# Edge scores of a graph attention layer: heads summed on TensorE by one-column products in place of ScalarE's summing passes

## What is computed

```python
out = (x @ Wv + bv)                        # V, 8 heads of 64
e = concat([x[src], x[dst]], axis=1) @ Ww + bw   # 6144 x 1024: 8 heads of 128
e = leaky_relu(e, 0.01)
w = (e @ Wa + ba)                          # Wa: 128 x 1, one score for each edge and head
mat = full((H, n, n), -inf).at[:, src, dst].set(w)
y = softmax(mat) @ out                     # then elu, residual, layernorm
```

## Time and profile before

| what | value |
|---|---|
| runs, median (lowest to highest) | 927.63 us (926.61 to 930.39) |
| the profiled execution, its own time | 931.85 us |
| its span, first to last instruction | 929.8 us |
| PE, busy share of the span | 72% |
| DVE | 59% |
| ACT | 29% |
| POOL | 25% |
| granted TensorE clock, mean | 0.825 |

### The profile page before, as it was taken

How to read it: one execution, slowest core, us unless ns; L and a number is a source line. 1 busy time by engine, 2 the same in 40 slices (tenths; PEclk the granted TensorE clock), 3 DMA queues, 4 the chain that set the end, 5 groups by cost and what they waited for, 6 DMA issues and landing times.

```text
span 929.8 us, 9900 instructions
## 1 busy us (share of the span) xinstructions
PE 664.9 (72%) x3019; PEld 336.2 (36%) x3053; DVE 544.3 (59%) x1452; ACT 273.2 (29%) x1097; POOL 231.4 (25%) x230
## 2 busy tenths in 40 slices
PE   5942443522317808972779989379999999999997
PEld 2421121201106704441355544234444444444442
DVE  2448986887978995448463242644458544444433
ACT  2105764645651312431131010202222222222222
POOL 4154776776852610000000000011110111111000
PEclk9985555755556958995879999769999999999999
DMA  8597576877749149003000000618999999999970
GB/s 336 206 389 271 161 250 210 248 222 238 231 158 336 57 170 406 35 0 136 1 0 1 0 1 0 233 39 331 399 401 398 392 395 401 396 388 400 387 292 36
DMA packets 46215, 208.04 MB, mean 224 GB/s; under 512 B 8128, under 2 KB 12224, under 8 KB 36560
## 3 DMA queue, kind: packets, MB, share of 16 engines
q1 hardware_dynamic: 26624, 145.43, 40.0%
q0 software_dynamic: 19536, 61.95, 20.3%
HBM read 200.45 MB, written 10.05 MB: 226 GB/s over the span
## 4 chain that ended last, share of the span: by engine, by line
PE 51%; DVE 8%; issue 1%; DMA 1%; ACT 1%; DVEq 0%; POOLq 0%
PE bank L781 13%; PE bank L809 7%; PE bank L801 6%; PE bank L693 4%; PE bank L708 3%; PE bank L514 2%; PE bank L615 2%; PE bank L621 2%; PE bank L770 2%; PE bank L509 2%; PE bank L762 1%; DMA R<-tok_tab,slot_tok 1%; PE bank L726 1%; PE bank L723 1%; DVE sm L1074 1%
## 5 line engine op out<-in xcount | busy, mean ns | idle before, releaser
L558 PE MATMUL bank<-R 128*128 128x384 bf16 x144 | 51.0, 490 | 140.5 <-DVE R L1156 110.7
L892 ACT ACTIVATE R<-R 128x128 f32<-128x128 f32 x384 | 113.3, 296 | 104.0 <-DVE R L1195 85.8
L781 PE MATMUL bank<-R 128*64 128x512 f32 x576 | 133.8, 607 | 0.0
L467 POOL DMA_INDIRECT R<-tok_tab,slot_tok x36 | 36.1, 1002 | 301.9 <-DVE slot_f L1546 301.2
L514 PE MATMUL bank<-R,xT_s 128*128 128x512 f32 x168 | 80.5, 640 | 1.9 <-DMA R<-L_Ww 1.9
L892 ACT ACTIVATION_READ_ACCUMULATOR R<-R 128x1 f32 x384 | 72.1, 188 | 13.7 <-issue 13.5
L558 PEld LDWEIGHTS bank<-R 128*128 128x128 bf16 x144 | 13.5, 120 | 173.2 <-DVE R L1156 129.1
L1558 DVE TENSOR_TENSOR R<-R,bank 128x256 f32<-128x256 f32 x36 | 15.1, 421 | 103.0 <-ACT R L972 103.0
L801 PE MATMUL bank<-R 128*64 128x512 f32 x288 | 73.3, 599 | 0.5 <-ACT R L966 0.5
L809 PE MATMUL bank<-R 128*128 128x512 bf16 x291 | 68.7, 379 | 6.3 <-issue 5.1
L427 POOL DMA_INDIRECT score<-w_e,e_i x48 | 59.4, 1238 | 41.7 <-DVE w_e L1150 29.6
(11 more groups left out here) (327 smaller groups left out, 1132.1 us busy)
## 6 DMA issues: line engine op xcount, KB each, us to landing
R<-L_w SPq DMA_DIRECT2D x72, 1536.0 KB, 10.1
R<-L_w SPq DMA_DIRECT2D x2, 3072.0 KB, 15.0
score<-R POOLq DMA_DIRECT2D x9, 512.0 KB, 14.7
R<-score SPq DMA_DIRECT2D x3, 1536.0 KB, 10.3
R<-L_Ww SPq DMA_DIRECT2D x2, 2048.0 KB, 14.6
R<-L_W SPq DMA_DIRECT2D x4, 1024.0 KB, 9.4
tab_src<-R SPq DMA_DIRECT2D x3, 516.0 KB, 2.7
tab_dst<-R SPq DMA_DIRECT2D x3, 516.0 KB
```

The source lines that it names most:

```text
L558: last = pe.matmul(pb[s][:, 0:N], oh[:, e % 2, 0, P * s:P * s + P], oh[:, e % 2, 1, :], start=(e == 0), stop=(e == ET - 1))
L781: last = pe.matmul(pb[4 + i % 2][halves[h], :], xeT[i % 2][:, k, halves[h]], w13[(2 * i + h) % NWB][:, k, :], start=(k == 0), stop=(k == K ...
L892: act_.activation(own, own, ACT.Copy, accum_out=w_e3[:, t, h:h + 1]).then_inc(S("heads_summed"), 1)
```

## The change

- **Tables** are plain: rows of 1024 numbers, `linear_part` and `add_linear` are gone. Target rows are built in three of the gather buffers (`ab_dst`), no longer in the buffers of the source rows.
- **DVE** rectifies in place, max(0.01 z, z) over 1024 columns, and later stores the sums of tile t-2 plus the bias from PSUM (`store_sums`).
- **PE** transposes the 8 heads of each tile (two banks of four), and sums a head by a product of the transposed head as weights with Wa, one column wide (`sum_heads`), one tile behind.
- **ACT** copies the two banks of transposes of each tile to SBUF (`leakyT`), 128x512 each, in place of its 8 passes.
- **V** is projected and gets its bias ahead of the loop. Wv and bv are loaded ahead of the table stores; gamma, beta and the two weights of the later layer after tile 10's scores.
- **Duplicates** are searched in groups of three tiles, each over its own and the previous tile (256 columns), in one bank; no search against the group before is needed.
- **POOL** gathers 10 tiles of source rows at once and four more in the first four tiles, into a ring of 14; a source buffer is free when its transposes are done. The scatter is of tile t-2.

```diff
-ROW = 2 * D + H
-NGF = 13
+ROW = 2 * D
+NGS = 14
+NGA = 10
 NGD = 6
-V_FROM = 4
+KEYS = 3
+Z_BANK = (3, 4, 5, 7)
...
+            sp.dma_start(Wv, a["L0_Wv"].rearrange(chunks, p=P)).then_inc(S("Wv_loaded"), 16)
+            sp.dma_start(bvr, a["L0_bv"].partition_broadcast(P)).then_inc(S("Wv_loaded"), 16)
...
+            sp.wait_ge(S("w_ready"), 10)
+            for row, name in ((g0r, "L0_gamma"), (b0r, "L0_beta")):
+                sp.dma_start(row, a[name].partition_broadcast(P)).then_inc(S("bit_w_loaded"), 16)
...
-                if t >= NGF:
-                    pool.wait_ge(S("rows_added"), t - NGD + 1)
+                if t >= NGS:
+                    pool.wait_ge(S("zT_psum"), 2 * (t - NGS) + 2)
...
             for t in range(ET):
-                if t >= 1:
-                    scatter_score(t - 1)
+                if t >= 2:
+                    scatter_score(t - 2)
                 if t + 4 < ET:
                     gather_dst(t + 4)
-                if NGF <= t + 4 < ET:
+                if t < NGS - NGA:
+                    gather_src(t + NGA)
+                if NGS <= t + 4 < ET:
                     gather_src(t + 4)
...
+            pe.wait_ge(S("Wv_loaded"), 32)
+            for t in range(NT):
+                project(t, 3 + t, xT, Wv).then_inc(S("V_psum"), 1)
...
+            def transpose_rows(t):
+                pe.wait_ge(S("leaky_ready"), t + 1)
+                for half in range(2):
+                    u = 2 * t + half
+                    if t >= 2:
+                        pe.wait_ge(S("leakyT_ready"), u - 3)
+                        if half:
+                            pe.wait_ge(S("w_ready"), t - 1)
+                    for j in range(4):
+                        o = D * half + P * j
+                        last = pe.transpose(pb[Z_BANK[u % 4]][:, P * j:P * j + P], ga[t % NGS][:, o:o + P], ident[:, :])
+                    last.then_inc(S("zT_psum"), 1)
+
+            def sum_heads(t):
+                pe.wait_ge(S("leakyT_ready"), 2 * t + 2)
+                for h in range(H):
+                    last = pe.matmul(pb[Z_BANK[(2 * t + 1) % 4]][:, h:h + 1], leakyT[(2 * t + h // 4) % 4][:, P * (h % 4):P * (h % 4) + P], wa,
+                                     start=True, stop=True)
+                last.then_inc(S("sums_psum"), 1)
...
             for e in range(ET):
+                transpose_rows(e)
                 pe.wait_ge(S("onehot_ready"), e + 1)
...
+                if e % KEYS == 1 and e // KEYS + 1 < ET // KEYS:
+                    edge_keys(e // KEYS + 1)
+                if e:
+                    sum_heads(e - 1)
...
-            for t in range(ET):
-                act_.wait_ge(S("prod_ready"), t + 1)
-                for h in range(H):
-                    own = prod[t % 2][:, P * h:P * h + P]
-                    act_.activation(own, own, ACT.Copy, accum_out=w_e3[:, t, h:h + 1]).then_inc(S("heads_summed"), 1)
+            for u in range(2 * ET):
+                act_.wait_ge(S("zT_psum"), u + 1)
+                if u >= 4:
+                    act_.wait_ge(S("sums_psum"), u // 2 - 1)
+                act_.activation(leakyT[u % 4], pb[Z_BANK[u % 4]][:, :], ACT.Copy).then_inc(S("leakyT_ready"), 1)
...
+            def store_sums(t):
+                dve.wait_ge(S("sums_psum"), t + 1)
+                ts(w_e3[:, t, :], pb[Z_BANK[(2 * t + 1) % 4]][:, 0:H], bar, None, ALU.add).then_inc(S("w_ready"), 1)
...
                 tt(ga[j], ga[j], gd[t % NGD], ALU.add).then_inc(S("rows_added"), 1)
                 dve.wait_ge(S("rows_added"), t + 1)
+                stt(ga[j], ga[j], SLOPE, ga[j], ALU.mult, ALU.max).then_inc(S("leaky_ready"), 1)
                 if t >= 2:
-                    dve.wait_ge(S("heads_summed"), H * (t - 1))
-                stt(prod[t % 2].rearrange(heads, h=H), ga[j][:, 0:2 * D].rearrange(heads, h=H), 0.0, bc(waR[:, None, :], [P, H, P]),
-                    ALU.max, ALU.mult).then_inc(S("prod_ready"), 1)
-                if t:
-                    add_linear(t - 1)
-            add_linear(ET - 1)
+                    store_sums(t - 2)
```

More of the change, by code:

```diff
@@ L400, in _ @@
             for q in range(9):
-                pool.dma_start(fill[q], ga[NGF - 1][:, 0:1024]).then_inc(S("score_filled"), 16)
+                pool.dma_start(fill[q], fill_s).then_inc(S("score_filled"), 16)
             pool.wait_ge(S("edge_idx_ready"), 1)
@@ L429, in scatter_score @@
                                         oob_is_err=False).then_inc(S(f"scores_stored{t % 2}"), 16)
-            for t in range(NGF):
+            for t in range(NGA):
                 gather_src(t)
@@ L538, in _ @@
             pe.wait_ge(S("dst_half_ready"), 2 * NT)
-            for e in range(ET):
[L540 to L554, removed]
+            pe.wait_ge(S("Wv_loaded"), 32)
@@ new lines, in _, with edge_keys @@
+            for t in range(NT):
+                project(t, 3 + t, xT, Wv).then_inc(S("V_psum"), 1)
+            def edge_keys(g):
+                if g:
+                    pe.wait_ge(S("dup_used"), g)
+                for j in range(KEYS + 1):
+                    e = KEYS * g + j - 1
+                    if e < 0:
+                        continue
+                    o = pb[6][:, P * j:P * j + P]
+                    pe.matmul(o, src_h[:, e:e + 1].to_broadcast([P, P]), ident16[:, 0:P], start=True, stop=False)
+                    last = pe.matmul(o, dst_h[:, e:e + 1].to_broadcast([P, P]), ident16[:, P:2 * P], start=False, stop=True)
+                last.then_inc(S("key_psum"), 1)
@@ L1112, in _ @@
             dve.engine_nop().then_inc(S("edge_idx_ready"), 1)
[L1113 to L1117, removed]
-            heads = "p (h c) -> p h c"
-            waL3 = bc(waL[:, None, :], [P, H // 2, P])
-            def linear_part(row, half, ready, bias=None):
-                own, o = lsc[:, D * half:D * half + D].rearrange(heads, h=H // 2), 2 * D + H // 2 * half
-                share = row[:, o:o + H // 2]
-                one(tt(own, row[:, D * half:D * half + D].rearrange(heads, h=H // 2), waL3, ALU.mult))
-                if bias is None:
-                    ins = dve.tensor_reduce(share, own, AX, ALU.add)
-                else:
-                    one(dve.tensor_reduce(share, own, AX, ALU.add))
-                    ins = ts(share, share, bias, None, ALU.add)
-                ins.then_inc(ready, 1)
-            for t in range(NT):
-                for half in range(2):
-                    dve.wait_ge(S("src_half_ready"), 2 * t + half + 1)
-                    linear_part(ab[t], half, S("src_rows_ready"))
-            for t in range(NT):
-                dve.wait_ge(S("src_rows_stored"), 16 * NT)
+            heads = "p (h c) -> p h c"
+            for t in range(NT):
                 dve.wait_ge(S("Ww_loaded_dst"), 32)
@@ L1190, in _ @@
-                dve.wait_ge(S(f"edge_rows{t % NGD}"), 16 * sum(1 if e < NGF else 2 for e in range(t % NGD, t + 1, NGD)))
+                    dve.wait_ge(S("first_src_rows"), 16 * NGA)
+                if t == NGA:
+                    dve.wait_ge(S("next_src_rows"), 16 * (NGS - NGA))
+                dve.wait_ge(S(f"edge_rows{t % NGD}"), 16 * sum(1 if e < NGS else 2 for e in range(t % NGD, t + 1, NGD)))
                 tt(ga[j], ga[j], gd[t % NGD], ALU.add).then_inc(S("rows_added"), 1)
                 dve.wait_ge(S("rows_added"), t + 1)
+                stt(ga[j], ga[j], SLOPE, ga[j], ALU.mult, ALU.max).then_inc(S("leaky_ready"), 1)
```

92 lines of the change are left out of this document (43 added, 49 removed).

## The result

The changed kernel takes 976.21 us (median of 4 runs, 975.55 to 980.03), the kernel before beside it 929.01 us (4 runs, 926.61 to 930.8): a ratio of 1.049, 95% interval 1.045 to 1.054. The change costs 47 us. The forecast was 948 us with a range from 908 to 980: the sign is right and the time lies in the range, but the loss is over twice the 20 us of the forecast. What came is close to the low end of the forecast's own clock estimate (971 us).

The account below looks back on a forecast made before the run. PE's turn, mixed from full and half clock, was taken to bound the changed loop: 4.64 us a tile, 223 us for 48 tiles, read back 20 us later, so 948 us against 927.63. The range was 908 to 980 us.

Parts of the forecast that it names:

- Ahead of the loop: Before the edge loop: PE projects V in 10.3 us, first rectified row at about 73.3 us, 2.6 us early.
- The prices on PE: PE's transposes, one-column products, one-hots and keys in a tile: 6.5 us at half clock, 3.3 at full.
- ScalarE: ACT in the loop: two copies of 0.60 us replace 8 passes a tile, its stalls taken as gone.
- The share at full clock: PE's clock in the loop: 60% of the time at full clock, ends 40% and 90%.
- the prediction's own formula: Loop pace: 3.9 us at full and 6.5 at half clock, mixed by share of time, giving 4.64 us a tile.
- The chain at full clock: DVE and PE waiting on each other in the loop: three tiles in 11.7 us, 3.9 a tile.
- rival 1: PE's clock holds full in the loop: 3.9 us a tile, 912 us in all; chance 20 in 100.
- POOL's turn: Three indirect transfers a tile in the loop: 4.2 us, hidden under PE's pace, at full clock the same as the chain.
- Rival 2: PE's clock stays half in the loop: 6.5 us a tile, +109 us, 1037 us in all; chance 10 in 100.

## Why the prediction came out as it did

**Ahead of the loop: right.** V's 24 records started at 58.84 and took 10.54 us, the first addition came at 71.97, the first rectified row ran from 73.23 to 74.46. The prediction put the end of that row at 73.3, so it was 1.2 us late. The first gather of target rows was issued from 64.16 to 65.09, where the prediction had the rows at hand by 65; when they landed isn't read here, but the first addition doesn't wait for them, so they didn't set the start, as foretold.

**The prices on PE: right.** A one-column record was put at 0.115 us at full and 0.22 at half clock; 1.90 / 16 = 0.119 and 3.52 / 16 = 0.22 came. The transposes were put at 0.92 and 1.75 us for eight; from their start to that of the one-hots it is 201.13 - 200.12 = 1.01 and 216.15 - 214.41 = 1.74. DVE's store of the scores was put at 0.15 us, where the row of before has 0.18; it takes 0.22. The Trainium skill (TensorE: Matmul & The Clock Gate, LDWEIGHTS) gives one figure for a weight load, 107 ns for 128 columns, with no clock in it; the 0.119 us at full clock is near it, the 0.22 us at half clock, twice that, speaks against it for f32, as the row of before did.

**ScalarE: right, and worth nothing here.** Its copies take 0.60 us, and its waits for nothing in the profile went from 31.6 us in 49 to 2.5 us in one. The 22.4 us that DVE had stood ahead of its store (18.7 for ACT, 3.7 without a releaser) became 77.3, of which 75.1 for PE.

**The share at full clock: the term that was wrong.** It was taken as 60% with ends of 40 and 90; it was 38%, just below the low end. Of the 28.0 us by which the profiled execution missed its forecast (980.03 against 952), 24.7 lie ahead of the read back (324.33 against 299.6), and this term carries them; 3.3 us lie behind it. By the prediction's own formula 40% gives 5.13 us a tile and +43 us; measured were 5.14 and +44.9 at the read back. So the mechanism was right and the share was mis-sized. No row of before showed such a mix, and the prediction chose 60% between ends that it could bound, leaning to the dense part of the tile because of the rise at 297 us. The rows that spoke for the low end stood beside it: the products that stayed at 0.50 from 280.88 on, first one-column and then 384-column ones. In the windows of 120 to 140 and 280 to 300 us of after PE was busy all the time without leaving 0.50. That PE is always busy was no sign of a high clock where half of its time went to one-column products; that their width is the cause of about half of the missing share is what the kernel with 64 columns shows (38 to 70%). The filler in PE's gaps adds another 12 points.

**The chain at full clock: right where it was seen, but not the floor.** 11.77 us for three tiles against 11.7. Over all kernels with eight f32 sums the formula, fed with the measured share, gives:

| kernel | share at full clock | pace by the formula | pace measured | measured minus formula, times 47 | DVE's waits without a releaser |
|---|---|---|---|---|---|
| after | 38% | 5.19 us | 5.14 us | -2 us | 0.4 us |
| 16 columns | 40% | 5.13 | 5.16 | +1 us | none |
| 64 columns, no source rows | 76% | 4.31 | 4.37 | +3 us | none |
| 64 columns | 70% | 4.43 | 4.74 | +15 us | 12.3 us |
| 64 columns and filler | 82% | 4.20 | 4.77 | +27 us | 26.9 us |

Two terms go a long way for the five kernels: the share, and the waits without a releaser, which the prediction didn't have and which are all but absent in after. For the kernel with the filler the agreement of 27 with 26.9 is partly luck, since the formula leaves out the time that the filler itself takes at half clock. A third term is the floor with PE off the bound: both such kernels with all their gathers, one head and bf16 sums, stop at 4.31 us, more than the 4.23 at which the change breaks even. POOL's own turn is close to that floor. The means of its scatter and two gathers over 72 to 280 us with three gaps of 0.3 give 1.47 + 1.07 + 0.96 + 0.9 = 4.4 us with one head and 1.30 + 1.15 + 1.03 + 0.9 = 4.4 with bf16 sums. With one head DVE does wait for its rows; with bf16 sums it waits mostly without a releaser, so there POOL's part isn't shown. So no run here shows that rival 1 (the clock holds full, 3.9 us a tile, 912 us) could be had: with the gathers in place no kernel here that sums on PE went below 4.31 over the loop. POOL's turn isn't a constant, either: the mean scatter is 1.24 us in before and 1.39 in after (L433 above), and the kernel before with V ahead of its loop ran at 4.12. The prediction had both numbers, 4.2 for POOL's turn and 3.9 for the chain, and wrote "at full clock it is the same as the chain"; taking the larger of the two would have left next to nothing of the faster outcome.

**Rival 2 (the clock stays half, 1037 us): no.** The clock was at full for 38% of the loop. The Trainium skill (same page, Part 4) says that the full clock doesn't engage for transposes, which don't count as PE-busy the same way. In the kernel with one head and no source rows the granted clock is 0.90 over 70 to 246 us, while the transposes are the largest part of PE's work:

```profile
L574 PE MATMUL bank<-ident,R 128*128 128x128 f32 x384 | 60.1, 306 | 75.6 <-DVE R L1201 70.7 <-issue 4.9
L592 PE MATMUL bank<-R 128*128 128x384 bf16 x144 | 35.8, 363 | 0.0
```

That speaks against the rule for f32 transposes. The one-hot products run beside them, but the kernel before with V ahead of its loop has the same one-hots without the transposes, and its clock stays at 0.50. The two loops differ in more than the transposes (traffic, pace, one head's sum), so it isn't shown by itself.

**What stays open.** What lets DVE and ScalarE go at the end of a wait without a releaser. These waits are there in the four kernels that run faster than after with all their gathers, and gone where the source rows are not gathered; in after and with 16 columns, with the same gathers, they are all but gone too. A single one each stands in the kernel before (3.7 us) and in the one with V ahead (6.7 us). Whether it is the traffic, the load on POOL or the number of instructions in so short a time, no run here separates. Whether such a stand makes the clock fall, or only goes with it, isn't settled either. What holds the bf16 kernel at 4.31 us stays open with it. And no kernel here that sums on PE and leaves no work out beats the one before: the bf16 sums come within 0.6% and are slower.

## What to carry to other kernels

A reduction over partitions by one-column f32 products costs PE a full weight load for one column of work, twice for each product, and at half clock twice again. Ask of such a stage what clock it will be granted before costing it at full clock. If the sums must go to PE and rounded operands will do, make them bf16: 0.40 us instead of 3.5 for eight at half clock. Where several engines have nearly the same pace (here POOL 4.2 to 4.4, the new chain 3.9, DVE 3.6 us a tile), the gain is bounded by the next one, and that bound is to be written down before the chances are.

## What the runs showed of the hardware

- 16 f32 records with 64 columns take 1.89 to 1.95 us at full clock, with one column 1.84 to 1.90: the 63 further columns cost 0.05 us for all 16. They raise the share at full clock from 38 to 70%; 16 columns don't (40%).
- A bf16 one-column record takes 0.34 / 8 = 0.043 us at full and 0.40 / 8 = 0.050 at half clock; an f32 one 0.12 and 0.22. The f32 product needs two of them, so the ratio is 8.8 at half clock, not 2.
- Less traffic and a lighter POOL went with a higher granted clock (48 to 80%) at a PE that was busy 58% of the time (101.89 of 176).
- PE, DVE and ScalarE stand together for 2 to 4 us with no releaser in the profile: 1.96 us from 145.15 with the filler, 4.19 us from 153.20 with bf16 sums. POOL issues the transfers already due meanwhile.
